# A cross-attention and mixture-of-experts layer on one core: where the last weights are asked for, and when probabilities are copied

## What is computed

```
x = x + attention(layernorm(x), ctx, ctx)      # x: 4 x 1024 x 256, ctx: 4 x 77 x 256, 16 heads of 64,
                                               # output projection, residual and a second layernorm inside
x = x + moe(layernorm(x))

moe(x): scores = softmax(x @ Wg)               # 32 experts
        weights, indices = top_k(scores, 4)    # 4096 tokens * 4 = 16384 pairs
        for each expert e: y[tok] += swiglu(x[tok], W1[e], W2[e], W3[e]) * w     # at most 2048 pairs each
        return y + swiglu(x, Ws1, Ws2, Ws3)    # the shared expert, for all tokens
swiglu(x, w1, w2, w3) = (silu(x @ w1) * (x @ w3)) @ w2
```

## Time and profile before

| | |
|---|---|
| time, median of 3 runs | 754.86 us (752.58 to 757.47) |
| the profiled execution's own time | 752.53 us |
| its span, first to last instruction | 750.8 us |
| busy, share of the span | PE 97%, PEld 76%, DVE 68%, ACT 61%, POOL 50% |
| mean granted TensorE clock | 0.999 |

### The profile page before, as it was taken

The page is one execution under the profiler, slowest core; times in us unless marked ns, Lnnn a source line. Parts: engine busy times, 40 slices in busy tenths (PEclk is TensorE's granted clock), DMA queues, the critical chain, the costliest instruction groups (busy, mean ns, idle before and its releaser), DMA issues.

```text
span 750.8 us, 18765 instructions
## 1 busy us (share of the span) xinstructions
PE 725.9 (97%) x4227; PEld 570.1 (76%) x4228; DVE 513.3 (68%) x1684; ACT 461.6 (61%) x1818; POOL 376.3 (50%) x373
## 2 busy tenths in 40 slices
PE   6998999999999999998999999999999999999997
PEld 4765777777777777775775578798999999999655
DVE  4865647385967868584879665566666666666798
ACT  2666777777786768776761426566666666666310
POOL 1002251325666666666467747765666666666300
PEclk9999999999999999999999999999999999999999
DMA  8721163323445454569937959987777777766997
GB/s 326 243 71 47 54 213 124 128 99 135 161 141 177 155 175 150 197 196 373 345 128 261 393 174 308 306 287 234 229 234 227 239 223 228 235 192 192 419 418 324
DMA packets 100847, 164.46 MB, mean 219 GB/s; under 512 B 11493, under 2 KB 82227, under 8 KB 99251
## 3 DMA queue, kind: packets, MB, share of 16 engines
q1 hardware_dynamic: 86911, 121.81, 49.3%
q0 software_dynamic: 13824, 41.96, 15.2%
q10 hardware_dynamic: 52, 0.01, 0.0%
HBM read 90.01 MB, written 78.97 MB: 225 GB/s over the span
## 4 chain that ended last, share of the span: by engine, by line
PE 73%; DVE 6%; DMA 5%; issue 5%; ACT 4%; POOL 3%; SPq 2%; DVEq 0%; ACTq 0%; POOLq 0%
PE psum L1897 15%; PE psum L1672 15%; PE psum L1775 15%; PE psum L1608 9%; PE psum L1904 7%; PE psum L1807 4%; DVE big L1569 4%; PE psum L1631 3%; ACT sm L974 2%; PE psum L1823 2%; DMA big<-y_d 2%; POOL expert_lists L809 2%; PE psum L1646 1%; PE psum L1639 1%; SPq L643 1%
## 5 line engine op out<-in xcount | busy, mean ns | idle before, releaser
L852 POOL DMA_INDIRECT y_d<-sm,yrow x160 | 153.9, 962 | 91.7 <-DVE yrow L1541 69.0
L1897 PE MATMUL psum<-xbT,w_now 128*128 128x128 f32 x1280 | 170.6, 276 | 1.7 <-issue 1.1
L974 ACT ACTIVATE sm<-psum,nmax 128x77 f32<-128x77 f32 x512 | 158.3, 372 | 4.5 <-DVE nmax L1188 4.4
L823 POOL TENSOR_TENSOR sm<-sm,sinv 128x1232 f32<-128x1232 f32 x32 | 71.9, 2247 | 177.1 <-DVE sinv L1195 177.0
L1897 PEld LDWEIGHTS psum<-xbT,w_now 128*128 128x128 f32 x1280 | 155.5, 192 | 5.0 <-issue 3.7
L809 POOL DMA_INDIRECT expert_lists<-rows,slot x128 | 125.4, 980 | 57.8 <-issue 35.3
L1775 PE MATMUL psum<-big,pT 128*128 (+1 forms) x640 | 143.5, 379 | 0.6 <-ACT pT L985 0.6
L1672 PE MATMUL psum<-big,xnT 128*128 (+2 forms) x384 | 138.9, 510 | 0.0
L1775 PEld LDWEIGHTS psum<-big,pT 128*128 128x128 f32 x640 | 119.1, 190 | 15.7 <-issue 0.8
L974 ACT ACTIVATION_READ_ACCUMULATOR sm<-psum,nmax 128x1 f32 x512 | 129.9, 254 | 0.0
L1672 PEld LDWEIGHTS psum<-big,xnT 128*128 128x128 f32 x384 | 70.0, 190 | 56.9 <-issue 51.3
(11 more groups left out here) (212 smaller groups left out, 944.8 us busy)
## 6 DMA issues: line engine op xcount, KB each, us to landing
xblk<-expert_lists SPq DMA_DIRECT2D x160, 160.0 KB
y_d<-zero SPq DMA_DIRECT2D x32, 512.0 KB
big<-y_d SPq DMA_DIRECT2D x8, 2048.0 KB, 17.2
big<-in_L_ffn_W SPq DMA_DIRECT2D x16, 320.0 KB
expert_lists<-expert_lists SPq DMA_DIRECT2D x32, 160.0 KB
xin<-in_x SPq DMA_DIRECT2D x36, 128.0 KB, 2.7
xres<-in_x SPq DMA_DIRECT2D x8, 512.0 KB, 5.6
x_d<-x SPq DMA_DIRECT2D x8, 512.0 KB, 2.7
```

The lines of the kernel that those rows point to most:

```text
L823: pool.tensor_tensor(e3, e3, sinv[:, t % 2, :].unsqueeze(2).to_broadcast([P, NH, SK]), ALU.mult).then_inc(s["probs_ready"], 1)
L852: pool.indirect_dma_start(out=y_d, out_offset=bass.IndirectOffsetOnAxis(ap=yrow[:, q:q + 1], axis=0), in_=eo[:, q, :], in_offset=None).the ...
L974: last = nc.scalar.activation(sm[:, t % 2, h * SK:(h + 1) * SK], head_scores(h, h + 1), ACT.Exp, bias=nmax[:, t % 2, h:h + 1], accum_out=s ...
L1897: last = mm(bank(2 + q % 2)[:, i * P:(i + 1) * P], w_now[:, q % 2, i, k, :], xbT[:, q % 2, k, :], start=k == 0, stop=k == KC - 1)
```

## The change

The diff has five parts. On ACT, `move_pT` is now ahead of the first half of `make_rows` in every group (so far in the last tile alone). On SP, the early `load_xg(0)`, `load_xg(1)` and `load_x2g(2)` move from ahead of group 7's steps to behind its steps 0, 1 and 2, and a wait is added ahead of those steps: `lists_ready[0]` must have reached 768, which is three groups of 256. On POOL, a group's scatters are split 5 and 3 over tiles 1 and 2 instead of 4 and 4. `AHEAD` is 6: one turn more, without fills beside it, is loaded before SP waits for the fills.

```diff
-    AHEAD = 5
+    AHEAD = 6
...
             for p in range(2):
                 sp.wait_ge(x2_stored[p], 16 * MID // 2)
-            load_xg(0)
-            load_xg(1)
-            load_x2g(2)
             sp.wait_ge(s["scores_psum"], (NT - 2 * TG) * SB)
             sp.wait_ge(s["out_psum"], NT - 2 * TG)
+
+            sp.wait_ge(lists_ready[0], 16 * TG * TOPK * (NG // 2 - 1))
             for t in range(TG):
                 load_experts(EARLY + (MIDDLE - EARLY) * t // TG, EARLY + (MIDDLE - EARLY) * (t + 1) // TG, "weights")
                 step(NG // 2 - 1, 1, t)
+                if t < 2:
+                    load_xg(t)
+                elif t == 2:
+                    load_x2g(2)
...
             load_turn(1, behind_second, second_row)
-            for i in range(2, AHEAD):
+            for i in range(2, AHEAD - 1):
                 load_turn(i, fill_lists(sp, fill_at_regs, (i - 1) * FILLS))
-            assert (AHEAD - 1) * FILLS == E and FILLS == NX and MID == 4
+            load_turn(AHEAD - 1)
+            assert (AHEAD - 2) * FILLS == E and FILLS == NX and MID == 4
             sp.wait_ge(s["filled"], 16 * E)
...
                 if t < 3 and live(jh, ph):
-                    scatter_rows(jh, ph, *((7 if live(j, p) else 5, 8), (8, 12), (12, 16))[t])
+                    scatter_rows(jh, ph, *((7 if live(j, p) else 5, 8), (8, 13), (13, 16))[t])
...
-                last_tile = isinstance(j, int) and num(j, p, t) == NT - 1
-                if t == 3 and live(*g1) and not last_tile:
-                    make_rows(*g1, (0, 1))
                 if live(jm, pm):
                     move_pT(jm, pm, tm)
-                if last_tile:
+                if t == 3 and live(*g1):
                     make_rows(*g1, (0, 1))
```

## The result

The changed kernel takes 773.18 us (median of 5 runs, 771.86 to 775.44) against 754.86 (752.12 to 757.47): a ratio of 1.0252, 95% interval 1.0224 to 1.0281. The forecast was 774, range 763 to 781. The profiled executions lie further apart than the medians (775.44 against 752.53): that of after is the slowest of its five, and that of before lies near the fastest of its.

What follows compares the result with a forecast made beforehand. PE was taken to set the pace nearly everywhere, unable to catch up later. +18.1 at s_up(2, 0), +1.2 for slow pace, -0.7 for the turn gave +18.6 us: median 754.9 to about 774, range 763 to 781.

Steps and rivals of the forecast that it cites:

- The opening of the last group: Tile opening the last group: with weights held back, ACT's wait for group 3's last scatter goes; gain of 3.0 us.
- ScalarE's order: Copying the probabilities ahead of the rows on ACT: no effect, work only changes places; at most 9 us lost.
- The first stall: SP's new wait delays tile 32's x, so PE's transpose_x in tile 31 stalls 15.1 us; net +12.1.
- The split: POOL's scatters 5 and 3: group 4's last one comes one scatter, 1.28 us, earlier; by itself no gain or loss.
- The second stall: Shared expert: load_x2g(0) lands late behind SP's queue, s_up(2, 0) starts at 432.3 instead of 414.23; +18.1 us in all.
- PE's pace after a stall: After an idle stall PE's matmuls run slowly; 1.2 us lost behind the second stall, the first's covered by the second wait.
- The turn without fills: Expert blocks: PE's wait for the first block after the last fill goes; gain of 0.7 us, bounds 0 and 3.0.
- The sum: Whole kernel: +18.1 (holding the 3.0 gained) + 1.2 - 0.7 = +18.6 us.
- What would be late next: Expert blocks: weights of experts 24 to 31 are asked for some 20 us later, hidden since PE needs them at 444 + 18.
- The rule: Issue a DMA early, wait late: by it alone the change only loses, 15.1 + 6.0 us; the trace adds the 3.0 gain.

Runs made afterwards that it cites:

- the profile of the turn without fills: Kernel before with only the sixth turn, without fills, loaded ahead (AHEAD 6); 753.62 us against 753.97, 0.9982.
- the kernel with the wait alone: Kernel before with only SP's new wait on the scatters of groups 0, 2 and 4 added; 770.61 us, 1.0228.
- the kernel with all but the weights ahead: Changed kernel with x loads, xn2T and x2 stores of tiles 28 to 31 and the three early loads ahead of the wait; 759.54 us, 1.0081.
- the loads of x ahead: Changed kernel with the loads of x for tiles 32 to 35 asked for ahead of the new wait; 772.0 us, 1.0239.
- the wait alone, in the kernel before: Kernel before with only an SP wait on the scatters of groups 1 and 3 added; 749.88 us against 753.97, 0.9945.

## Why the prediction was right, point by point

- **The opening of the last group: +3.0 foreseen, 2.9 measured** (14.37 - 11.49). Its cause is shown from both sides: in the kernel before, the weights held until group 3's scatters have landed give it, and so, in part, does an order that puts other work into ScalarE's wait. What I left out is that the clock can fall behind the wait (15.60 us in the profile of the turn without fills).
- **ScalarE's order: right as a sum, for half of the reason.** With the weights held it is worth next to nothing (11.63 and 11.49 without and with it). I only asked what it could lose. Where the scatter is late it covers some of the wait, 1.8 us of the opening's window; that it would be a gain without the rest of the change I missed. I also wrote that in every other group the window shows no wait: I had read only one. The opening of group 6 took 12.08 us with PE busy for 11.38 (296.08 to 308.16).
- **The first stall: net +12.1 foreseen.** 390.61 - 377.16 - 1.33 = 12.1. Each step holds: SP on at 379.1 (380.66 - 1.33 = 379.3), the load 3.0 later (3.21), landing 6.2 (6.3), a wait of 14.8 (15.1). The split counts as foreseen, about one scatter: SP goes on 40.75 us after the start of tile 28 (380.66 - 339.91), and 42.03 after it in the kernel with the wait alone (379.81 - 337.78), though the order differs there too. What I left out is the store of `xn2T`, a second transfer behind the same wait with the same price; it is hidden as long as the load of x is late as well, and would have spoilt any repair of the load alone.
- **The second stall: +18.1 foreseen at `s_up(2, 0)`, 435.90 - 414.23 - 1.33 = +20.3 measured.** This term was undersized, at one step: I let 4.3 us for the three moved loads cancel against a quicker SP. From the load of tile 32 to that of tile 35 SP took 33.25 us, not 29.6. The kernel with the wait alone tells the two apart: without the three loads SP took 27.72, so it was quicker by 1.9 only, and the three loads added 5.5. The two issues took 0.8 longer, the landing 8.8 instead of 6.9 + 4.3: 3.65 + 0.8 - 2.4, and 0.2 from SP's start. That the second wait is a time of SP's queue, not of PE, is shown by the kernel with all but the weights ahead: PE comes to it at 410.2 instead of 430.5, and waits 8.67 instead of 5.38 for a load that SP could ask for only behind the weights, at 406.20.
- **PE's pace after a stall: 1.2 foreseen, 1.9 measured** behind the second (5.50 us for eight matmuls against 3.60 in the earlier trace rows), and 2.0 behind the first (6.52 against 4.49 for the same twenty), which the second wait swallows, as argued. The trace now shows the clock too, which it didn't at the start. The windows (length, busy PE, then the granted clock; 0.50 is the lower of its two levels, 1.2 of 2.4 GHz) before and after the first stall:

```profile
376.00:390.60 14.60, 0.00 (x0) 0.57 0.68 220
390.60:394.00 3.40, 3.39 (x9) 0.50 1.11 313
394.00:397.00 3.00, 3.00 (x12) 0.80 0.96 271
397.00:400.00 3.00, 2.82 (x18) 1.00 1.06 377
```

That is what the Trainium skill, TensorE: Matmul & The Clock Gate, Part 1, says of an idle array. Here it cost 1.7 and 1.8 us behind waits of 2.7 and 4.5 us (the wait alone; the loads of x ahead), 1.9 behind 5.4, 2.6 behind 8.7 (everything but the weights ahead), each time in the eight matmuls of `s_up(2, 0)`, and 2.0 behind 14.8.
- **The turn without fills: 0.7 foreseen, not settled.** The two profiles differ by 0.67 from the first block to the end (306.62 and 305.95), which looks like it, but the other kernels differ by as much among themselves, so it can't be read so.
- **The sum.** 20.3 + 1.9 - 0.7 = 21.5 in the profiled pair against 18.6 foreseen, 18.3 in the medians. The medians agree better than the terms, in part by luck: of the 22.9 between the two profiled executions 1.33 lies ahead of tile 28, and single runs of the kernel before lie 5 us apart here and 9 in the last session (751.43 to 760.18).
- **What would be late next.** I wrote that the weights of experts 24 to 31 can come 20 us later at no cost. They came 26 later (426.77 against 400.88), and the windows of the blocks are those of before. The weights of experts 5 to 23, put behind `load_x2g(1)`, cost 15 us, by the block loads behind them, not by their own deadline.
- **The rule** of the Trainium skill (DMA: Bandwidth & Descriptors, Rules for kernel authors: issue early, wait late) speaks against every hold. The runs differ for a short one: 8 us of hold gained 2.7 us in the opening's window and 4.1 in the medians (the wait alone, in the kernel before); 49 us cost 18, as the rule has it.

## What to carry to other kernels

A wait put into a queue's order is priced by what stands behind it, not by what it guards: list every later issue on that engine, the stores that free a buffer included, with the time by which each is needed; in these kernels the largest lateness counted, not the sum. Wait for the event that the measured stall names (here the last scatters of group 3, in ScalarE's row) and for no later one. And two edits that reach for the same wait are to be counted once.

## What was not expected of the hardware

The profiled execution of after lost time where the change is far away. About 72 us from its start the granted clock fell to the lower of its two levels and came back (columns: length, busy PE, clock, DMA share, GB/s); in the execution of before all these windows show 1.00:

```profile
70.00:72.00 2.00, 1.26 (x7) 0.74 0.08 23
72.00:74.00 2.00, 2.00 (x7) 0.50 0.99 296
74.00:76.00 2.00, 2.00 (x6) 0.91 0.90 303
72.00:85.00 13.00, 13.00 (x54) 0.91 0.42 138
```

Just ahead of it, at the end of the set-up, PE waited for ACT three times, 0.81, 0.65 and 1.21 us. In the execution of before it waited for the same three times as long, and the clock stayed. The 14 us up to the scores of tile 2 and tile 2 itself took 14.06 and 10.58 us against 13.20 and 9.77 before: 1.67 us. The profile of the turn without fills has it as well (14.00 and 10.64), besides the fall of the clock in its last group's opening. Why the clock falls behind such short waits in some executions and not in others isn't known; it is a reason not to read 1 or 2 us from the spans of two profiles, but from the windows in which the edit works, with the clock beside them.
